# A fused two-stack transformer kernel: the transfers of the turned probabilities go ahead of v's, one wait is narrowed, the output product changes its PSUM bank, and the engines' written orders change

## What is computed

```python
x = x + 0.5 * _L0_ffn_ref(_layernorm(x), ...)      # stack 0, six layers
x = x + _L0_attn_ref(_layernorm(x), ...)           # the middle part
x = x + 0.5 * _L0_ffn_ref(_layernorm(x), ...)      # stack 1, six layers
# in a stack, DEPTH = 6:
for i in range(DEPTH):
    x = attn_layer(shift_tokens(x), Wqkv[i], q_scale[i], k_scale[i], Wo[i]) + x
    x = ffn_layer(shift_tokens(x), ln_g[i], ln_b[i], W1[i], b1[i], W2[i], b2[i]) + x
```

## Time and profile before

| | |
|---|---|
| median of 3 runs | 3517.3 us (3502.58 to 3526.32) |
| profiled execution | 3534.39 us, of it the span of instructions 3532.6 us |
| TensorE matmul | 3108.0 us, 88% of the span |
| VectorE | 2935.2 us, 83% |
| GpSimd | 2429.1 us, 69% |
| ScalarE | 2115.4 us, 60% |
| DMA | 343.41 MB, mean 97 GB/s |
| granted TensorE clock | 0.976 of full speed (mean) |

### The profile page before, as it was taken

How to read it: one execution, slowest core, us unless ns; L and a number is a source line. 1 busy time by engine, 2 the same in 40 slices (tenths; PEclk the granted TensorE clock), 3 DMA queues, 4 the chain that set the end, 5 groups by cost and what they waited for, 6 DMA issues and landing times.

```text
span 3532.6 us, 118084 instructions
## 1 busy us (share of the span) xinstructions
PE 3108.0 (88%) x50214; PEld 2417.3 (68%) x50214; DVE 2935.2 (83%) x3356; ACT 2115.4 (60%) x2794; POOL 2429.1 (69%) x1229
## 2 busy tenths in 40 slices
PE   7889898899988999888887898998898898898888
PEld 5767777777777777765333677777777677677777
DVE  6878888887888888886998888888888888888885
ACT  5556556565566556557776556555565565565655
POOL 6767677676676776662998768667667667667663
PEclk8999999999999999999999999999999999999999
DMA  3434344344344443431100434434434434434432
GB/s 112 119 97 106 104 108 117 98 113 118 96 110 119 106 108 92 103 97 31 39 0 13 119 90 106 123 90 111 122 96 108 122 95 104 116 99 107 106 88 80
DMA packets 247413, 343.41 MB, mean 97 GB/s; under 512 B 41005, under 2 KB 139886, under 8 KB 246894
## 3 DMA queue, kind: packets, MB, share of 16 engines
q1 hardware_dynamic: 246894, 335.85, 36.3%
HBM read 35.80 MB, written 1.05 MB: 10 GB/s over the span
## 4 chain that ended last, share of the span: by engine, by line
PE 43%; SPq 25%; DMA 8%; issue 7%; DVE 7%; ACT 5%; POOL 4%; DVEq 0%; ACTq 0%; POOLq 0%
SPq L1995 15%; PE PS L427 12%; DMA ARENA<-PB 8%; SPq L1975 6%; PE PS L237 3%; PE PS L588 3%; PE PS L453 3%; PE PS L373 3%; PE PS L238 3%; PE PS L239 3%; SPq L1973 2%; PE PS L532 2%; PE PS L304 2%; PE PS L534 2%; PE PS L533 2%
## 5 line engine op out<-in xcount | busy, mean ns | idle before, releaser
L1821 POOL TENSOR_TENSOR ARENA<-ARENA 128x1024 f32<-128x1024 f32 x192 | 471.0, 2453 | 458.9 <-DVE ARENA L1388 457.7
L427 PEld LDWEIGHTS PS<-ARENA 128*64 128x64 f32 x12288 | 405.6, 146 | 241.8 <-DMA ARENA<-PB 181.6
L427 PE MATMUL PS<-ARENA 128*64 128x64 f32 x12288 | 435.9, 233 | 153.3 <-DMA ARENA<-PB 140.1
L1829 POOL TENSOR_TENSOR ARENA<-ARENA,RN 128x1024 f32<-128x1024 f32 x192 | 365.1, 1901 | 295.3 <-ACT RN L984 288.5
L237 PE MATMUL PS<-WL,XH 128*128 128x512 f32 x1152 | 512.4, 445 | 44.9 <-DVE ARENA L1388 34.7
L1063 ACT ACTIVATE ARENA<-PS 128x1024 f32<-128x1024 f32 x192 | 196.3, 1023 | 515.0 <-PE PS L427 515.0
L304 PE MATMUL PS<-C,ARENA 128*128 128x128 f32 x3120 | 410.8, 277 | 94.9 <-issue 63.9
L238 PE MATMUL PS<-WH,XL 128*128 128x512 f32 x1152 | 461.8, 401 | 0.0
L239 PE MATMUL PS<-WH,XH 128*128 128x512 f32 x1152 | 461.4, 401 | 0.0
L1815 POOL TENSOR_TENSOR ARENA<-ARENA 128x1024 f32<-128x1024 f32 x192 | 455.3, 2371 | 7.0 <-DVE ARENA L1370 7.0
L304 PEld LDWEIGHTS PS<-C,ARENA 128*128 128x128 f32 x3120 | 348.8, 142 | 132.6 <-issue 102.1
(11 more groups left out here) (166 smaller groups left out, 6446.8 us busy)
## 6 DMA issues: line engine op xcount, KB each, us to landing
ARENA<-ARENA SPq DMA_DIRECT2D x576, 256.0 KB, 4.2
ARENA<-PB SPq DMA_DIRECT2D x1488, 64.0 KB
ARENA<-ARENA SPq DMA_DIRECT2D x384, 128.0 KB, 2.7
ARENA<-in_wqkv SPq DMA_DIRECT2D x36, 512.0 KB, 4.8
ARENA<-in_wo SPq DMA_DIRECT2D x12, 512.0 KB, 4.0
ARENA<-in_w SPq DMA_DIRECT2D x12, 341.0 KB, 4.2
ARENA<-in_w SPq DMA_DIRECT2D x12, 192.0 KB, 4.6
QKS<-in_qks SPq DMA_DIRECT2D x12, 128.0 KB, 2.4
```

Of the source, the lines that this page charges most:

```text
L427: last = nc.tensor.matmul(out.rearrange("p (a q) -> p a q", a=2)[:, :, col:col + 32], v2[:, win, hp, :], pt[:, :, win, hp, :], start=True, ...
L1821: nc.gpsimd.tensor_tensor(KN[n % 2], KN[n % 2], T2, ALU.add).then_inc(k_add, 1)
```

## The change

SyncE calls `spread_probs(n - 1)` before `spread_values(n)`. The tail transfer of v counts on a semaphore of its own, `tail_in`, and the other four on `v2_in`, which now reaches 64 for a tile. `v_evacuate(n)` waits for the tail transfer of tile n - 1 and for the four others of tile n - 2. `values` waits for all five, through the new helper `spread_ready`.

`out_project` writes bank 6 (the scores' slot 3) in the steady part and not bank 2; `residual` reads it there. With this the waits for a free slot move: `out_project` waits until the scores of two tiles later are subtracted (`sub_done` of s - 21), the scores and `ffn_up1` wait for `residual` of tile s - 23, and `k_transpose` waits for the carried keys and the layer norm's logarithm.

The written orders of TensorE, ScalarE, VectorE and GpSimd change as the diff shows. No instruction is added or removed, and no shape changes. The last tiles (`finish_tiles`) keep their order; the three waits there take the helper `spread_ready`, and are left out below.

```diff
@@ -163,7 +163,7 @@
         w1_in, inw_in, mw_in = sem("w1_in"), sem("inw_in"), sem("mw_in")
-        v2_in = [sem(f"v2_in{i}") for i in range(2)]
+        v2_in, tail_in = [sem(f"v2_in{i}") for i in range(2)], sem("tail_in")
         eps_set, pad_set, zero_set, masks_set, edge_set, tab_set, floor_set = (sem(n) for n in (
@@ -327,17 +327,17 @@
                     pe.wait_ge(b_add, n // NT + 1)
-                after_tile(pe, res_done, s - 23)
+                after_tile(pe, car_ev, s - 20)
                 if (s - 25) % 4 == 3:
...
                 if (s - 24) % 4 == 3:
+                    after_chunk(pe, f_ln, (s - 24) // 4)
                     after_chunk(pe, f_xm, (s - 24) // 4)
...
                     after_chunk(pe, f_ln, (s - 23) // 4 - 1)
-                    after_tile(pe, car_ev, s - 20)
                     after_chunk(pe, f_h[2], (s - 24) // 4 - 1)
@@ -398,8 +398,9 @@
                     after_chunk(pe, f_h[1], (s - 24) // 4)
-                after_tile(pe, sub_done, s - 21)
+                after_tile(pe, res_done, s - 23)
                 if s < RAMP or s >= N:
+                    after_tile(pe, sub_done, s - 21)
                     after_chunk(pe, f_h[1], (s - 23) // 4 - 1)
@@ -429,6 +430,10 @@
 
+            def spread_ready(n):
+                pe.wait_ge(tail_in, 16 * (n0 + n + 1))
+                pe.wait_ge(v2_in[n % 2], 64 * ((n0 + n) // 2 + 1))
+
             def probs_ready(n):
@@ -439,7 +444,7 @@
                 probs_ready(n)
-                pe.wait_ge(v2_in[n % 2], 80 * ((n0 + n) // 2 + 1))
+                spread_ready(n)
                 s = n + 22
@@ -461,15 +466,11 @@
                 s = n + 23
-                if (s - 24) % 4 == 3:
-                    after_chunk(pe, f_ln, (s - 24) // 4)
-                after_tile(pe, car_ev, s - 20)
+                after_tile(pe, sub_done, s - 21)
                 if s < RAMP or s >= N:
-                    after_chunk(pe, f_ln, (s - 23) // 4 - 1)
-                    after_chunk(pe, f_h[2], (s - 24) // 4 - 1)
-                    after_tile(pe, kT_ev, s - 21)
+                    after_chunk(pe, f_h[1], (s - 24) // 4 - 1)
                     after_tile(pe, res_done, s - 24)
-                out_products(n, 2)
+                out_products(n, 6)
 
@@ -732,21 +734,21 @@
                 k_project(s - 19)
+                k_transpose(s - 20)
+                q_transpose(s - 20)
                 out_project(s - 23)
-                q_transpose(s - 20)
-                k_transpose(s - 20)
                 ffn_up0(s - 24)
...
                 v_project(s - 20)
+                ffn_centre(s - 23)
+                carry(s - 19)
+                bias_products(s - 20)
                 scores(s - 20)
-                bias_products(s - 20)
-                carry(s - 19)
-                ffn_centre(s - 23)
+                ffn_variance(s - 23)
                 ffn_down(s - 24)
                 values(s - 22)
-                ffn_variance(s - 23)
                 p_transpose(s - 21)
@@ -988,7 +990,9 @@
                 if n:
-                    act.wait_ge(v2_in[(n - 1) % 2], 80 * ((n0 + n - 1) // 2 + 1))
+                    act.wait_ge(tail_in, 16 * (n0 + n))
+                if n >= 2:
+                    act.wait_ge(v2_in[n % 2], 64 * ((n0 + n) // 2))
                 if n == 1:
@@ -1162,25 +1166,25 @@
                 ffn_high(s - 23)
+                q_evacuate(s - 19)
+                k_evacuate(s - 19)
                 split_k(s - 18)
                 exponentials(s - 20)
-                q_evacuate(s - 19)
-                k_evacuate(s - 19)
+                gelu1(s - 23)
                 gelu0(s - 23)
-                gelu1(s - 23)
+                gelu2(s - 23)
                 q_square(s - 17)
-                gelu2(s - 23)
-                split_input(s - 24)
                 restore_tables(s - 23)
+                ffn_square(s - 22)
+                carry_evacuate(s - 18)
                 v_evacuate(s - 19)
                 inverse_norms(s - 18)
-                carry_evacuate(s - 18)
-                ffn_square(s - 22)
+                split_input(s - 24)
                 ffn_rsqrt(s - 22)
+                split_v(s - 19)
                 o_evacuate(s - 21)
...
                 k_square(s - 17)
-                split_v(s - 19)
                 split_q(s - 17)
@@ -1454,8 +1458,9 @@
                 dve.wait_ge(wo_done, n0 + n + 1)
-                nc.vector.tensor_tensor(B[0:64, q0:q0 + 128], PSB[0:64, 2, 0:128], A[0:64, q0:q0 + 128], ALU.add)
-                nc.vector.tensor_tensor(B[64:128, q0 + 1:q0 + 129], PSB[64:128, 2, 0:128], A[64:128, q0 + 1:q0 + 129],
+                o = PSB[:, 6 if n < N - 4 else 2, 0:128]
+                nc.vector.tensor_tensor(B[0:64, q0:q0 + 128], o[0:64, :], A[0:64, q0:q0 + 128], ALU.add)
+                nc.vector.tensor_tensor(B[64:128, q0 + 1:q0 + 129], o[64:128, :], A[64:128, q0 + 1:q0 + 129],
                                         ALU.add).then_inc(res_done, 1)
@@ -1567,23 +1572,23 @@
                     w1_low(0)
+                k_rotate2(s - 19)
                 residual(s - 23)
-                k_rotate2(s - 19)
                 k_sums(s - 19)
-                floor_sums(s - 19)
                 row_sums(s - 21)
                 gate0(s - 24)
+                floor_sums(s - 19)
+                gate2(s - 24)
                 gate1(s - 24)
-                gate2(s - 24)
                 q_rotate1(s - 18)
...
                 turn_probs(s - 21)
+                q_sums(s - 18)
+                fold_bias(s - 20)
+                ffn_normalise(s - 23)
                 row_max(s - 20)
-                q_sums(s - 18)
                 ffn_residual(s - 24)
-                ffn_normalise(s - 23)
                 subtract_max(s - 20)
-                fold_bias(s - 20)
                 k_rotate1(s - 18)
@@ -1874,16 +1879,16 @@
                     low_input(3)
+                w_low_k(s - 18)
                 ffn_low(s - 23)
...
                 p_normalise(s - 20)
-                w_low_k(s - 18)
+                k_normalise(s - 18)
                 q_normalise(s - 18)
                 q_add_halves(s - 17)
-                k_normalise(s - 18)
+                input_low(s - 24)
                 w_low_q(s - 17)
                 w_low_v(s - 19)
-                input_low(s - 24)
             k_add_halves(95)
@@ -1969,7 +1974,7 @@
                 last, v = (VT[i % 2].rearrange("p (a c) -> p a c", a=2) for i in (n - 1, n))
-                sp.dma_start(v2[0:64, 0, :], last[96:128, :, :]).then_inc(v2_in[n % 2], 16)
+                sp.dma_start(v2[0:64, 0, :], last[96:128, :, :]).then_inc(tail_in, 16)
                 sp.dma_start(v2[64:128, 0, :], v[0:32, :, :]).then_inc(v2_in[n % 2], 16)
@@ -2010,8 +2015,8 @@
             for n in range(N):
+                spread_probs(n - 1)
                 spread_values(n)
-                spread_probs(n - 1)
                 l, T = divmod(n, NT)
```

More of the change, by code:

```diff
@@ L630, in finish_tiles @@
                 tile(sub_done, 94)
-                pe.wait_ge(v2_in[1], 80 * ((n0 + 93) // 2 + 1))
+                spread_ready(93)
                 value_products(93)
@@ L652, in finish_tiles @@
                 probs_ready(94)
-                pe.wait_ge(v2_in[0], 80 * ((n0 + 94) // 2 + 1))
+                spread_ready(94)
                 value_products(94)
@@ L666, in finish_tiles @@
                 probs_ready(95)
-                pe.wait_ge(v2_in[1], 80 * ((n0 + 95) // 2 + 1))
+                spread_ready(95)
                 value_products(95)
```

## The result

The changed kernel takes 3382.11 us, the median of 4 runs (3371.71 to 3402.91), against 3517.24 us before: a ratio of 0.9627 (95% interval 0.9569 to 0.9686). Forecast were 3350 us, with 3265 to 3470 as the range. Run twice more beside other kernels it had ratios of 0.9656 (0.9627 to 0.9686) and 0.9641 (0.9613 to 0.9669). Its profiled execution spans 3401.1 us, 131.5 us less than the one before.

The account below looks back on a forecast made before the run. The prediction took a loop of the product of values, SyncE's issues and P's transfers as the bound. Four tiles fall from 66.1 to 62.3 us (2 x 13.6 + 14.6 + 20.5); 44 groups save 167 us: 3517 to 3350, range 3265 to 3470.

Parts of the forecast that it names:

- P ahead of v: SyncE's queue: P's transfers start 3.54 us sooner, their loop falls from 13.96 to 10.4 us, both waits for P go.
- V's copy and the tail: ScalarE's copy of v waits for the tail transfer alone: a loop of 12.8 us with a 3.3 us landing.
- slower rival: The tail's landing stretches behind P's eight transfers, deciding from 5.7 us; 3609 us at 6.4; chance 0.06.
- Plain tiles: Two turns in four: floor 13.0 us from VectorE, plus 0.6, gives 13.6 us, a gain of 1.1 each.
- Centre turn: Turn with the layer norm's centre: TensorE's work, now with the variance, gives 14.6 us, a gain of 0.1.
- Up turn: Turn with the up products: variance and output product's wait leave it; 20.5 us against 22, a gain of 1.5.
- 0.4 for layer changes + 0.6 for new waits: Allowances in the turn with the up products, added to 19.5 us to give 20.5 us.
- Output product, transposes first: Output product in bank 6 starts later; residual and k_rotate2 behind it wait 0 to 0.4 us, within the 0.6.
- P's waits under 30 us: Sign: the product of values and VectorE's turn of P each wait below 30 us for P's landings.
- No 100 us for the tail: Sign: waits of over 100 us by v's copy for the tail would mean that the tail's loop binds.
- The last gate's wait: Sign: VectorE's 2.91 us wait at its last gate in the up turn is gone.
- stays at 21.5: Sign of a wrong forecast: the turn with the up products stays at 21.5 us.

Follow-up runs that it names:

- e1: Changed kernel with v's five transfers issued ahead of P's eight again: 3489.77 us, 0.9946 of the kernel before.
- e2: Kernel before the change with only P's transfers put first and v's copy waiting for the tail alone: 3506.57 us, 1.0006 of the kernel before.
- e3: Changed kernel in which v's copy waits for all five transfers of the tile before, not the tail alone: 3820.61 us, 1.0894 of the kernel before.
- e4: Changed kernel with the layer norm's variance product behind the product of values again, on TensorE alone: 3450.05 us, 0.983 of the kernel before.
- e11: Changed kernel with TensorE's output product ahead of the two transposes again: 3781.2 us, 1.0753 of the kernel before.
- e9: Changed kernel with all loads of later layers' weights in up turns and v's transfers laid between P's: 3333.62 us, 0.9488 of the kernel before.

## Why the prediction was right, step by step

**P ahead of v.** Right that both waits for P go and that SyncE's queue leaves the chain; e1 shows the loop to be worth some 100 us with the new orders. The prediction gave it a gain of its own, 1.1 us in each plain turn; alone it brings none: e2 is at 1.0006.

**V's copy and the tail.** I took a landing of 3.3 us behind P's transfers. In the changed kernel it is

```profile
DMA to landing us min/median/max: 2.6/2.6/4.3
```

so transfers ahead of it did not stretch it, and v's copy waits 12 us in all. The slower rival decided at 5.7 us and is out of reach. e3 confirms the loop. With P's landings at 2.1 us in the median, the rule of the Trainium skill (DMA: Bandwidth & Descriptors, "Queues, rings and completion order") that a semaphore's increment follows every earlier write of its DMA engine asks for no more than these 2.6 us; the trace agrees, but doesn't test it.

**Plain tiles.** Forecast 13.6 us each; measured 12.1 and 14.0, together 1.1 less. VectorE's 12.93 us were no floor for a single turn: after the long up turn it has less to do, 10.37 us of the one shown above, and the first plain turn falls to TensorE's 12.0.

**Centre turn.** Forecast 14.6; measured 15.6. Those without stops take 14.3 in the median. The rest are mostly stops (1.2 us on average in the turn that ends with tile 0 of a layer, 2.3 with tile 12).

**Up turn.** Forecast 20.5; measured 21.7. Both named gains are real: e4 gives them back, turns without stops are at 19.2 us (21.5 before) and the output product no longer waits for its input. What was mis-sized is "0.4 for layer changes + 0.6 for new waits". Up turns at a layer's change take 24.8 us, some 4 over the others, by a stop and the clock after it.

**The step that fell short** is thus the term for new waits: I looked for them in semaphores, 0.6 us in the up turn, and found them within TensorE's own products, 121 us of stops more in 174 tiles, some 2.8 us in four. Four tiles gained 2.7 us, not 3.8: 121 us in 174 tiles, and the rest of the execution, which I had put at nothing, gave the other 10 us of the 131.5.

**What I put at nothing, and luck.** Bank 6 and the transposes' new place were in the prediction as a cost alone. That k's transposes waited for the residual ("issue" at L304: 63.9 us in 139 places, 13.7 in 5 after; 56.1 in e2, which has the old bank and orders, 11.7 in e1, which has the new) I hadn't seen; it is a gain of the other sign than the stops, as the first plain turn's is. The total is 32 us from the forecast in part because such errors offset each other. That is luck and not the sum's merit.

**Output product, transposes first.** The margin of a few tenths held: the residual waits for the output product 25.6 us in all (15.3 before). The order is worth more than the margin shows: e11 costs 390 us.

**Signs.** P's waits under 30 us: yes. Plain turns 13 to 14: their mean, 13.1, is. No 100 us for the tail: yes. The last gate's wait: VectorE's gates wait 50.3 us in all (150.6 before), at most 2.4, so mostly. The plain turns stayed under 14.3 us, the second by 0.3 only. The up turn "stays at 21.5": by the mean, 21.7 us, this sign of a wrong forecast came. Of the term it stands for, the 2.3 us that turns without stops gained are there; stops and layer changes took them back.

## What to carry to other kernels

When a wait is removed from an engine that is nearly full, ask what the wait was covering, its instruction stream included: short instructions back to back (here 400 in 3.6 us, weight loads included) use up what was brought ahead, and large transfers in flight seem then to keep the next packet away. Look for pauses within one line of a profile, but first make sure that the line is not that of two calls: between two calls a pause can be a wait that the profile doesn't name, and the end of another engine's instruction 0.10 us before gave it away here. And a loop of transfers and a loop of engine orders of about the same length must be shortened together: each alone was worth 0 to 16 us here, both 120.

## What the runs showed of the hardware that I had not expected

TensorE's instructions come in 16 KB packets, one for every 256 matmuls and weight loads, on the 16 DMA engines that move the data; halving 1 MB a tile of SBUF traffic took 65 us of stops and 100 us of time away (more than the stops; v's transfers also land sooner, and no run parts the two). From the start of a late packet to the next instruction passes 2.46 us in the median. Within a stop of 4.2 us the granted clock fell to 0.50, stayed there for the 5.4 us of work behind it, and was 1.00 again after. The kernels that wait more show a lower clock on the whole: a mean of 0.932 in e3 and 0.958 in e11, against 0.984 in e9.
